# Attention scores on TensorE: batch stacks without padding in two row halves, two batches' matmuls issued alternately

## What is computed

```python
Q, K = _rope(heads(Wq)), _rope(heads(Wk))          # layer 0
def attend(q, k):
    s = (q k^T + LAMBDA * (q*q)(k*k)^T) * inv_sqrt_d
    s = where(causal, s, -1e9)
    return softmax(s) @ V
out1, out2 = attend(Q, K), attend(_rotate_half(Q), _rotate_half(K))
...
attn = einsum('bnhd,bmhd->bnmh', q, k) * scale      # layer 1
w = softmax(attn, axis=2); y = w @ v
```

## Time and profile before

| | us |
|---|---|
| median of 3 runs | 392.0 |
| lowest, highest | 389.99, 392.19 |
| span of the profiled execution | 390.1 |
| steady phase of layer 0 (one batch) | 20.83 |
| steady phase of layer 1 | 17.51 |

### The profile page before, as it was taken

The page is one execution under the profiler, slowest core; times in us unless marked ns, Lnnn a source line. Parts: engine busy times, 40 slices in busy tenths (PEclk is TensorE's granted clock), DMA queues, the critical chain, the costliest instruction groups (busy, mean ns, idle before and its releaser), DMA issues.

```text
span 390.1 us, 9779 instructions
## 1 busy us (share of the span) xinstructions
PE 324.2 (83%) x3088; PEld 228.7 (59%) x3088; DVE 269.5 (69%) x694; ACT 242.0 (62%) x539; POOL 188.0 (48%) x475
## 2 busy tenths in 40 slices
PE   3866389889899999999878789899999999998645
PEld 2644267668676766777555457556565656665323
DVE  2999788885758676766544775787787968785123
ACT  5565627775656647565663145777869686878812
POOL 3677628794656564655673100025353442426330
PEclk9999768999999999999998869999999999999985
DMA  8565441120121212122200000110011110101000
GB/s 242 193 146 159 146 101 43 45 63 24 43 70 43 68 41 68 41 67 45 64 9 27 2 28 24 39 34 24 23 34 39 31 45 21 34 3 30 3 13 13
DMA packets 23364, 21.31 MB, mean 55 GB/s; under 512 B 3104, under 2 KB 20384, under 8 KB 23328
## 3 DMA queue, kind: packets, MB, share of 16 engines
q1 hardware_dynamic: 23328, 20.86, 19.0%
HBM read 13.24 MB, written 7.34 MB: 53 GB/s over the span
## 4 chain that ended last, share of the span: by engine, by line
PE 32%; DVE 21%; issue 16%; POOL 16%; ACT 7%; DMA 4%; SPq 3%; POOLq 1%; DVEq 1%; ACTq 0%
PE bank L974 6%; DVE NM L733 6%; PE bank L1023 4%; PE bank L1030 4%; POOL PB L429 3%; DVE XN L679 2%; PE bank L951 2%; POOL GA L464 2%; POOL RS L369 2%; POOL GA L468 2%; ACT PB L554 2%; DVE STAT L669 2%; DMA xs<-in_x 2%; DVE TQ L686 2%; POOL HELD L427 2%
## 5 line engine op out<-in xcount | busy, mean ns | idle before, releaser
L733 DVE TENSOR_REDUCE NM<-bank 128x3 f32<-128x384 f32 (+1 forms) x256 | 150.5, 613 | 47.5 <-PE bank L924 31.5
L554 ACT ACTIVATE PB<-bank 128x384 f32<-128x384 f32 (+1 forms) x256 | 136.0, 553 | 49.4 <-PE bank L953 27.9
L951 PE MATMUL bank<-QS,KS 128*128 128x256 f16 x256 | 71.0, 279 | 12.4 <-ACT PB L554 10.5
L974 PE MATMUL bank<-PB,VP 128*32 128x256 f32 (+1 forms) x1024 | 61.7, 358 | 7.1 <-POOL PB L429 5.6
L429 POOL TENSOR_SCALAR_AFFINE_SELECT PB<-PB 128x256 f32<-128x256 f32 x128 | 52.8, 413 | 0.0
L427 POOL TENSOR_TENSOR HELD<-EPSC 128x1 f32<-128x1 f32 x128 | 26.0, 203 | 54.5 <-ACT PB L554 53.0
L974 PEld LDWEIGHTS bank<-PB,VP 128*32 128x32 f32 x1024 | 26.7, 109 | 30.8 <-POOL PB L429 9.2
L951 PEld LDWEIGHTS bank<-QS,KS 128*128 128x128 f16 x256 | 25.0, 98 | 25.5 <-ACT PB L554 18.9
L927 PE MATMUL bank<-KS,QS 96*128 96x256 f16 x128 | 36.4, 285 | 2.3 <-issue 1.9
L464 POOL TENSOR_TENSOR GA<-TH,GS 128x256 f32<-128x256 f32 x21 | 18.2, 867 | 40.6 <-ACT GS L613 39.1
L924 PE MATMUL bank<-KS,QS 96*128 96x256 f16 x128 | 36.9, 289 | 0.0
(11 more groups left out here) (104 smaller groups left out, 678.2 us busy)
## 6 DMA issues: line engine op xcount, KB each, us to landing
scr<-PR SPq DMA_DIRECT2D x16, 256.0 KB, 2.3
QS<-scr SPq DMA_DIRECT2D x16, 128.0 KB, 2.7
QS<-scr SPq DMA_DIRECT2D x32, 64.0 KB, 2.8
KS<-scr SPq DMA_DIRECT2D x32, 64.0 KB, 2.7
KS<-scr SPq DMA_DIRECT2D x16, 128.0 KB, 3.0
scr<-PR SPq DMA_DIRECT2D x16, 128.0 KB, 1.9
QS<-MT SPq DMA_DIRECT2D x64, 4.0 KB
out_x<-xs SPq DMA_DIRECT2D x8, 128.0 KB, 1.9
```

The source lines that it names most:

```text
L554: act.activation(PB[s % RING][:, 0:n], TB_[s % 2][:, 0:n], ACT.Exp).then_inc(s_e[L], 1)
L733: dve.tensor_reduce(NM[p][:, s, 0:n], SB_[score_bank(s)][:, 0:w].rearrange("q (n k) -> q n k", n=n), AX.X, ALU.max, negate=True).then_inc( ...
L951: pe.matmul(o[:, 0:S], k[:, 0:P], q[:, :], start=True, stop=True)
L974: ins = pe.matmul(o, v, pr, start=(g % 2 == 0 and kt == 0), stop=True, skip_group_check=True)
```

## The change

The stacks are no longer one per parity but one per layer, of 128 partitions: batches of even number use partitions 0 to 63, odd ones 64 to 127 (`HALF * p`). A matmul of scores reads only the filled rows (`ROWS`: 48 or 24), one of shifted scores two more, where the maxima and ones stand. No zeros are needed; ones are filled once over the whole of KS by POOL at the start. The mask is split in two, since a half has only 64 rows for 128 rows of mask: `mask(..., 0)` covers the upper 64 rows of a block over 128 columns, `mask(..., 1)` the lower 64 over 64 columns. Where a phase has next scores, `both` issues the two batches' matmuls alternately.

```diff
-        QS = [[sb(f"QS{L}{p}", [P, H, S], F16) for p in range(2)] for L in range(2)]
+        QS = [sb(f"QS{L}", [P, H, S], F16) for L in range(2)]
...
-                for dst, src in ((QS[L][p][0:R, cs], sq[:, cs]), (QS[L][p][R:R + h, cs], sq[0:h, cs]),
+                o = HALF * p
+                for dst, src in ((QS[L][o:o + R, cs], sq[:, cs]), (QS[L][o + R:o + R + h, cs], sq[0:h, cs]),
...
             def first_stack(L, b, stored):
-                sp.wait_ge(s_init[L][b], 4 if L else 2)
-                sp.wait_ge(s_ones[L], (1 + L) * (b + 1))
+                sp.wait_ge(s_ones[L], 1)
                 sp.wait_ge(s_scr[L][b], stored)
...
-            ones_0(0)
+            for L in range(2):
+                pool.memset(KS[L][:, :, :].rearrange("q h t -> q (h t)").bitcast(U32), TWO_ONES).then_inc(s_ones[L], 1)
...
-                                clear_ones(b, s // 10)
...
-            clear_0(0)
...
-            clear_0(1)
...
-                            fill(KS[1][b][0:MROW, cs].rearrange("q h t -> q (h t)").bitcast(F32), 0).then_inc(s_init[1][b], 1)
...
-                            dve.memset(QS[1][b][:, cs].bitcast(U32), 0).then_inc(s_init[1][b], 1)
...
+            def score(L, p, s, part):
+                rows = slice(HALF * p, HALF * p + ROWS[L])
+                q, k, o = QS[L][rows, s], KS[L][rows, s], SB_[score_bank(s)]
...
+            def shift(L, p, s, part):
+                rows = slice(HALF * p, HALF * p + ROWS[L] + 2)
+                q, k, o = QS[L][rows, s], KS[L][rows, s], TB_[s % 2]
...
+            def both(L, b, p, s):
+                n, m = b + 1, 1 - p
+                o = SB_[score_bank(s)]
+                score_waits(L, n, s)
+                if L == 0:
+                    mask(m, o[:, 0:P], 0)
+                    shifted_waits(L, b, s)
+                    shift(L, p, s, 0)
+                    mask(m, o[:, 0:P], 1)
+                    score(L, m, s, 0)
+                    shift(L, p, s, 1).then_inc(s_t[L], 1)
+                    mask(m, o[:, 2 * P:3 * P], 0)
+                    mask(m, o[:, 2 * P:3 * P], 1)
+                else:
+                    score(L, m, s, 0)
+                    shifted_waits(L, b, s)
+                    shift(L, p, s, 0)
+                ins = score(L, m, s, 1)
+                ins.then_inc(s_s[L], 1)
+                if L == 1:
+                    shift(L, p, s, 1).then_inc(s_t[L], 1)
...
                 def phase(b, p, with_scores, later):
                     for s in range(H):
                         if with_scores:
-                            scores(L, b + 1, 1 - p, s)
-                        shifted(L, b, p, s)
+                            both(L, b, p, s)
+                        else:
+                            shifted(L, b, p, s)
```

More of the change, by code:

```diff
@@ L41 @@
 HC = H // 2
+HALF = P // 2
 LAM = 0.1
@@ L47 @@
 QSCALE = 1.0 / float(np.sqrt(HD))
-MROW = 96
+ROWS = (48, 24)
 RING = 8
@@ L125, in program @@
         VP = [sb(f"VP{p}", [P, TPB, H * 32]) for p in range(2)]
-        QS = [[sb(f"QS{L}{p}", [P, H, S], F16) for p in range(2)] for L in range(2)]
-        KS = [[sb(f"KS{L}{p}", [P, H, S], F16) for p in range(2)] for L in range(2)]
+        QS = [sb(f"QS{L}", [P, H, S], F16) for L in range(2)]
+        KS = [sb(f"KS{L}", [P, H, S], F16) for L in range(2)]
         PB = [sb(f"PB{n}", [P, 2 * S]) for n in range(RING)]
@@ L152, in program @@
         s_out = sem("out_stored")
-        s_init = [[sem(f"stacks_cleared_{L}{p}") for p in range(2)] for L in range(2)]
         s_ones = [sem("stack_ones_0"), sem("stack_ones_1")]
@@ L288, in load_max @@
                 for n in range(2):
-                    sp.dma_start(QS[L][p][MROW + n:MROW + n + 1, HC * c:HC * (c + 1), :],
+                    row = HALF * p + ROWS[L] + n
+                    sp.dma_start(QS[L][row:row + 1, HC * c:HC * (c + 1), :],
                                  MT[p][c][:, n, :]).then_inc(s_mi[L][c], 16)
@@ L912, in _, with score_waits @@
             pe.wait_ge(s_msk, 1)
-            def scores(L, b, p, s):
+            def score_waits(L, b, s):
                 if s % HC == 0:
@@ L918, in scores, with mask @@
                     pe.wait_ge(s_mx[L], at(16, b, bank_free(s)))
-                q, k, o = QS[L][p][0:MROW, s], KS[L][p][0:MROW, s], SB_[score_bank(s)]
-                if L == 0:
[L921 to L925, removed]
-                else:
-                    pe.matmul(o[:, 0:S], q[:, 0:P], k[:, :], start=True, stop=True)
-                    ins = pe.matmul(o[:, S:2 * S], q[:, P:2 * P], k[:, :], start=True, stop=True)
+            def mask(p, o, part):
+                rows = slice(HALF * p, HALF * (p + 1))
+                if part == 0:
+                    pe.matmul(o, MSK[rows, 0:P], MSK[rows, 2 * P:3 * P], start=True, stop=True, skip_group_check=True)
+                else:
+                    pe.matmul(o[:, HALF:P], MSK[rows, P:2 * P], MSK[rows, 3 * P:3 * P + HALF], start=False, stop=True,
+                              skip_group_check=True)
@@ new lines, in score @@
+            def score(L, p, s, part):
+                rows = slice(HALF * p, HALF * p + ROWS[L])
+                q, k, o = QS[L][rows, s], KS[L][rows, s], SB_[score_bank(s)]
+                if L == 0:
+                    if part == 0:
+                        return pe.matmul(o[:, 0:P], q[:, 0:P], k[:, 0:P], start=False, stop=True, skip_group_check=True)
+                    return pe.matmul(o[:, P:3 * P], q[:, P:2 * P], k[:, :], start=False, stop=True,
+                                     skip_group_check=True)
+                return pe.matmul(o[:, part * S:(part + 1) * S], q[:, part * P:(part + 1) * P], k[:, :], start=True,
+                                 stop=True)
@@ new lines, in shifted_waits @@
+            def shifted_waits(L, b, s):
+                if s % HC == 0:
+                    pe.wait_ge(s_mi[L][s // HC], at(32, b, 32))
+                if s >= 2 or not (isinstance(b, int) and b == 0):
+                    pe.wait_ge(s_e[L], at(16, b, s - 1))
+            def shift(L, p, s, part):
+                rows = slice(HALF * p, HALF * p + ROWS[L] + 2)
+                q, k, o = QS[L][rows, s], KS[L][rows, s], TB_[s % 2]
+                if L == 0 and part:
+                    return pe.matmul(o[:, S:S + P], k[:, P:2 * P], q[:, P:2 * P], start=True, stop=True)
+                return pe.matmul(o[:, part * S:(part + 1) * S], k[:, part * P:(part + 1) * P], q[:, :], start=True,
+                                 stop=True)
@@ new lines, in scores, with shifted @@
+            def scores(L, b, p, s):
+                o = SB_[score_bank(s)]
+                score_waits(L, b, s)
+                if L == 0:
+                    mask(p, o[:, 0:P], 0)
+                    mask(p, o[:, 0:P], 1)
+                ins = score(L, p, s, 0)
+                if L == 0:
+                    mask(p, o[:, 2 * P:3 * P], 0)
+                    mask(p, o[:, 2 * P:3 * P], 1)
+                ins = score(L, p, s, 1)
+                ins.then_inc(s_s[L], 1)
+            def shifted(L, b, p, s):
+                shifted_waits(L, b, s)
+                shift(L, p, s, 0)
+                ins = shift(L, p, s, 1)
+                ins.then_inc(s_t[L], 1)
@@ L943, in max_rows @@
                              IDF[:, :]).then_inc(s_mt[L], 1)
[L945 to L956, removed]
             def pv(L, b, p, g):
@@ L1192, in _program_inputs @@
     upper = np.triu(np.ones((P, P), np.float32), 1) * np.float32(-1e30)
-    masks = np.stack([np.eye(P, dtype=np.float32), upper, upper.T], 1)
+    one = np.tile(np.eye(HALF, dtype=np.float32), (2, 1))
+    none = np.zeros_like(one)
+    masks = np.concatenate([one, none, none, one, np.tile(upper[0:HALF], (2, 1)), np.tile(upper[HALF:, HALF:], (2, 1))], 1)
     return {"x": c(a["L0_attn_x"]), "w0": c(w0), "tab": c(tab), "small": c(small), "w1": c(w1), "wint": c(wint),
```

31 lines of the change are left out of this document (9 added, 22 removed).

## The result

| | before | after |
|---|---|---|
| median, us | 392.1 (4 runs) | 434.3 (4 runs) |
| lowest, highest | 389.99, 392.23 | 427.64, 443.97 |
| profiled execution | span 390.1 | 431.56, span 429.8 |
| mean granted clock of TensorE | 0.950 | 0.822 |

After takes 1.103 times as long as before [1.096, 1.111]. The prediction was 385.5, range 371 to 404: wrong in sign, and outside the range. The ratios compare each kernel's fast executions alone, of after 427.64 and 431.56 us; the slower ones, left out, stand at lower clocks (436.96 us at 0.804, 443.97 at 0.792), and two of the nine executions of before beside e1 took 424.7 us at 0.74 and 1015.6 at 1.00.

A forecast was written before the change was run, and what follows sets the result against it. PE, paced by the columns it streams, was taken as the bound. Terms 0 (layer 0), -7.7 (layer 1), -2.0 (fills), +1.2 (first scores), +2.0 (passage, unpaired phases) gave -6.5 from the median 392.0: 385.5 us, range 371 to 404.

The forecast's parts named there:

- a granted clock of 0.5 in the steady phases: Last listed sign that the prediction is wrong; the trace of before has 1.00 there.
- Heads: TensorE's head time: layer 0 falls 0.11 to 0.34 us, layer 1 falls 0.22 to 0.22 us, halves overlapping.
- the rival against that: Row halves don't overlap because matmuls wait for their predecessor; about 419 us, chance 0.08.
- Changes of tile shape: Added passages between small tiles and full array around tails and PV, 0.095 us each, bounds 0 and 0.2.
- the rival that they cost more: Tile-shape changes at every tail of the steady phases cost over 0.095 us; at 0.15, 398 us; chance 0.19.
- Layer 0 steady, taken as 0: Batches 2 to 6 of layer 0: -1.8 us from heads plus 18 x 0.095 for changes gives -0.1, taken as 0.
- Layer 1, -1.1 a phase: Second stretch of layer 1's phases: heads save 2.2 us, 12 added changes cost 1.1; seven phases give -7.7.
- the third rival: Waits take the gain: both puts the exp wait ahead of next scores; 393 us, or 389; chance 0.21.
- the fourth rival: DVE becomes the bound: layer 1 phase falls to DVE's 14.1 us if the chain shortens; 369 us, chance 0.12.
- Fills, -2.0: Batches 0 and 1 of layer 0 lose the clearing of layer 1's stacks: 0 to 3.6 us, taken 2.0.
- First scores, +1.2: Scores without partner at the start, at 1.2 GHz: 128 more columns, 0.11 us a head, over 11 heads.
- Passage and phases without pairs, +2.0: Some 53 added tile-shape changes there, 5.0 us, partly in PE's idle time; taken 2.0, bounds 0 and 5.

The follow-up runs named there:

- e1: The changed kernel with both batches' stacks in partitions 0 to 63, so no two matmuls run side by side; 548.6 us, 1.40 times before, clock 0.652.
- e5: The changed kernel with stacks widened by rows of zeros (QS) or ones (KS) to 62 and 64 rows, still side by side; 409.1 us, 1.048 times before.
- e10: e5 with 48 and 50 rows in both layers in place of 62 and 64; 412.8 us, 1.056 times before, clock 0.903.
- e6: e1 (halves not side by side) with 62 and 64 rows, QS filled with zeros beforehand; 461.3 us, 1.182 times before, clock 0.841.
- e4: The kernel before, padded full-array stacks kept, with only the alternating order of both and its place of the wait; 393.9 us, 1.008 times before.
- e2: The changed kernel with scores and then shifted scores in place of both, waits in the old places; 430.8 us, 1.102 times before.
- e8: The kernel before with KS filled whole with ones and the stacks' fills moved to idle time in the first 12 us; 389.5 us, 0.997 times before.
- e7: The kernel before with MROW 65 in place of 96: scores on 65 rows, shifted scores on 67, full array, some fills gone; 400.2 us, no ratio.
- e9: e8 with MROW 126 in place of 96: scores read 126 rows, shifted scores 128 as before; 387.6 us, 0.997 times before.

## Why the prediction was wrong

**The step that failed** is one that was never priced: every term of the sum was worked out with the clock of the trace of before. The text named "a granted clock of 0.5 in the steady phases" last among the signs of an error, and had no rival and no chance for it. Yet it had the lower level in its own rows: 0.76 in the passage and 0.11 us for 128 columns at the first scores, and took it for a property of those places. The change cuts the rows of the commonest matmuls from 96 and 128 to 24 and 26 in layer 1, and to 48 and 50 in layer 0. The runs showed a granted clock of 0.58 to 0.93 in seven of after's phases of batches 1 to 6, 0.62 in the passage (before 0.84) and 0.822 in all, and a time of 434.3 us. Widening the matmuls to 62 and 64 rows (e5) gave back 22.7 of the 39.7 us by which the spans differ (429.8, 390.1; e5 407.1). Most of it lies in layer 1, 13.5 us, where the tile's height changed with the rows, so which of the two counts there isn't shown; in layer 0, where only the rows changed, it is 4.5 us side by side (5.1 against e10) and 10.2 one after another (e6 against e1). The 17 us that e5 is still over before stand in the table: 5.6 at the start, in which e5 also fills more; 4.3 in layer 0; 4.5 in the passage, at a clock of 0.74 against 0.84; 1.0 and 1.6 in the rest.

**Heads**: right. 0.35 for 0.34 us in layer 0, 0.23 for 0.22 in layer 1; a 64-column matmul 0.03; the halves run side by side, so the rival against that falls, though its 419 lies nearest of all to the result. A time that is nearly hit doesn't confirm its mechanism: here the heads were short and the clock was down.

**Changes of tile shape**: 0.095 us each holds where a row shows one (0.09 behind the head at 322.77). The phase at 319.20 has 23 of them, as counted; 19 of their gaps hold no wait or other pause and add up to 1.8 us, 0.095 each, so the rival that they cost more falls.

**Layer 0 steady, taken as 0**: +0.6 to +0.7 us a phase at full clock (21.40 against 20.83; batch 5 alone 21.38 against 20.69). The exchange of head for changes, -0.1, is not what missed: in batch 5 PE is busy 19.18 us, before 19.14. Its waits grow from 1.4 to 2.0 us. The order is part of it: on the full array it costs 0.3 to 0.5 (e4), and it was priced at nothing; with the halves and the old order batch 5 takes 21.16 (e2), so 0.2 go with the order there and 0.5 with the rest.

**Layer 1, -1.1 a phase**: -0.3 (17.20 against 17.51), and less than 0.1 where several phases in a row are at 1.00 (17.45 in e5 and 17.47 in e10). Waits took the gain, as in the third rival, but not for its reason: with the waits back in the old places the phase is the same, 17.14 us (e2). The waits of PE for the exp in batch 3 (319.25 to 336.40), and then in batch 3 of before (291.26 to 308.76):

```profile
PE bank L909 <- ACT PB L519: 1.7, 3, 0.9
```
```profile
PE bank L951 <- ACT PB L554: 0.9, 2, 0.8
```

With three waits of 0.2 us each for DVE and ACT that before doesn't have, PE waits 1.4 us more, and most of what the faster heads save turns into wait (in e2 the exp's wait is 1.4). Overlap is worth 0.9 us a phase (e6 against e5), not PE's 3.5: PE was no longer what bounds all of the phase. DVE, the fourth rival, had 13.88 of 17.20 us and didn't become the bound.

**Fills, -2.0**: 1.9 in e8. **First scores, +1.2**: the first PV came 2.6 us later than before; after's clock from 44 to 64 us was 0.51, before's from 46 to 62 us 0.65:

```profile
44.00:64.00 20.00, 13.92 (x130) 10.65 (x130) 14.38 (x31) 5.20 (x12) 6.00 (x22) 0.51 0.38 95
```

**Passage and phases without pairs, +2.0**: +7.9 in the passage and +5.9 at the end. e5 has as many changes of shape, +4.5 at 0.74 and +1.6, so at most that is theirs.

Had the clock stayed, the sum by these terms (an estimate from the rows above) would have been near 5 x 0.7 in layer 0, less 7 x 0.05 to 0.35 in layer 1, less 1.9, plus 1 to 3 for the start (priced 1.2, measured 2.6) and 2 to 5 for the passage (priced 2.0, at most e5's 4.5): some 2 to 9 us slower than before. By this estimate the change had no gain to lose even without the clock, and the clock is some 31 to 38 of the 39.7 us.

What stays open: what exactly brings the clock down. In layer 1 rows and the height of the tile weren't told apart: a run with 30 and 32 rows in layer 1, its tiles still 32 high, would be a first test. Rows alone don't order all runs. After and e1 have the same matmuls, and after, with its halves side by side, has phases at 1.00 where e1 has 0.50 without a break; e10's layer 0 drops to 0.93 in batches 2 and 4 with 48 and 50 rows side by side where e6's, with 62 and 64 one after another, is at 1.00 in batches 3 to 5, and yet at 0.50 in batches 0 and 1. Why a phase of after is at 0.58 and the next, of the same work, at 1.00 isn't settled either.

## What to carry to other kernels

Zero rows that widen a matmul are not waste to be cut unseen: the contraction rows cost nothing in time at a given clock (a steady phase of layer 1 is 17.5 us with scores on 65, 96 and 126 rows: e7, before, e9), and cutting them here, with the smaller tiles that came of it, took the clock from TensorE. Before packing small matmuls into row groups, ask what the engine's clock will be with so few rows in use, and give a fall to the lower level a price and a chance, above all where a trace already shows the lower level in its thinner stretches. When a changed kernel is slower, read the clock by stretch before looking for a wait.

## What was not expected of the hardware

- TensorE without idle time for 30.8 us, on 24 and 26 rows, is granted 0.50 throughout (e1); a phase of layer 1 on 62 and 64 rows takes 18.3 us at 1.00 (e6). But e6 also has a phase of layer 0 on 62 and 64 rows, 30.58 us without idle time, at 0.50.
- Added rows whose products are zero bring the clock back: layer 0 from +9.4 (e10) to +4.3 us (e5) by them alone; layer 1, batch 2, from 0.58 to 1.00 by them or the higher tile.
- In full-array mode too: 65 and 67 rows for 96 and 128 stood at 0.79 for 1.00 in one phase of the one profile, 17.5 us for 14.3 (e7).
- Two row halves side by side: starts at most 0.01 us apart, also at the lower level, and without alternating issue: the third matmul issued starts with the first (e2).
